# Paired row maxima in three PSUM banks: another grouping and order of the fills in causal attention heads

## The reference

```
score = einsum('bhqd,bhkd->bhqk', Q, K) / sqrt(8)
score = score - 1e10 * (1 - causal);  score = score - max(score, axis=-1)
weights = softmax(score);  attn = einsum('bhqk,bhkd->bhqd', weights, V)
```

## Time and profile before

| | |
|---|---|
| median of 3 runs | 1905.73 us (1902.89 to 1910.19) |
| profiled execution, its own time | 1905.62 us |
| its span, first to last instruction | 1903.8 us |
| mean granted clock of TensorE in it | 0.928 of full speed |
| the heads of layer 3 in the span | about 1403 to 1834 us |
| busy over the span | TensorE 87%, VectorE 75%, ScalarE 59% |

### The profile page before, as it was taken

One profiled execution on the slowest core, in us unless ns is written; L12 is line 12 of the kernel. 1 busy time (PEld: TensorE's weight loads), 2 busy tenths in 40 slices (PEclk: granted clock), 3 DMA queues, 4 the chain that ended last, 5 costly groups with the idle time before them and its releaser, 6 DMA issues. The chain is left out here.

```text
span 1903.8 us, 29255 instructions
## 1 busy us (share of the span) xinstructions
PE 1647.4 (87%) x10137; PEld 663.2 (35%) x10137; DVE 1428.8 (75%) x2698; ACT 1114.0 (59%) x2266; POOL 311.3 (16%) x462
## 2 busy tenths in 40 slices
PE   2899999999999995889997797893559998999987
PEld 1412222222222222434444544782322222323256
DVE  5689999999999944665555507656768999999825
ACT  3168888888888883332222244452206777777754
POOL 0101200000000100000000345543011222111123
PEclk8879999999999997899997899997658999999999
DMA  4101211121110012023223269951421111111132
GB/s 124 48 20 49 78 59 48 47 75 61 51 47 29 24 35 63 21 68 109 94 89 145 70 201 325 305 180 38 178 72 44 47 47 44 44 49 51 37 83 72
DMA packets 77378, 155.66 MB, mean 82 GB/s; under 512 B 17572, under 2 KB 34852, under 8 KB 73536
## 3 DMA queue, kind: packets, MB, share of 16 engines
q1 hardware_dynamic: 62630, 123.96, 20.1%
q0 software_dynamic: 14384, 29.29, 5.1%
q10 hardware_dynamic: 218, 0.55, 0.1%
HBM read 103.41 MB, written 48.89 MB: 80 GB/s over the span
## 5 line engine op out<-in xcount | busy, mean ns | idle before, releaser
L859 ACT ACTIVATE heads_probs<-heads_pS 128x512 f32<-128x512 f32 (+3 forms) x1664 | 819.8, 578 | 182.3 <-PE heads_pS L771 96.2
L883 DVE TENSOR_REDUCE heads_run_max<-heads_pM 128x1 f32<-128x1024 f32 x512 | 601.3, 1219 | 26.5 <-PE heads_pM L746 18.1
L790 PE MATMUL heads_pO<-heads_probs,heads_vh 128*32 128x512 f32 (+2 forms) x3328 | 445.9, 583 | 0.7 <-ACT heads_probs L859 0.7
L746 PE MATMUL heads_pM<-heads_ks,heads_qs 56*128 56x512 bf16 (+3 forms) x1040 | 319.5, 380 | 20.1 <-DVE heads_run_max L894 9.4
L771 PE MATMUL heads_pS<-heads_qs,heads_ks 59*128 59x512 bf16 (+3 forms) x1040 | 306.1, 368 | 2.4 <-DMA heads_qs<-heads_max_rows 1.6
L894 DVE TENSOR_REDUCE heads_run_max<-heads_pM 128x1 f32<-128x512 f32 x384 | 246.6, 684 | 16.5 <-PE heads_pM L746 14.2
L746 PE MATMUL heads_pM<-heads_k_first,heads_q_first 56*128 56x512 bf16 x624 | 193.2, 384 | 30.1 <-DVE heads_run_max L923 15.8
L771 PE MATMUL heads_pS<-heads_q_first,heads_k_first 59*128 59x512 bf16 x624 | 188.8, 377 | 4.6 <-ACT heads_probs L859 4.6
L771 PEld LDWEIGHTS heads_pS<-heads_qs,heads_ks 59*128 59x128 bf16 x1040 | 81.8, 93 | 266.9 <-ACT heads_probs L859 232.7
L891 DVE CUSTOM_DVE_ANT_0 heads_masked_out<-heads_pM,heads_mask_end 128x128 bf16<-128x128 f32 (+3 forms) x256 | 121.2, 486 | 13.1 <-PE heads_pM L746 8.2
L1410 ACT ACTIVATE top_act_gate<-top_pG 128x512 f32<-128x512 f32 x68 | 40.6, 597 | 137.2 <-PE top_pU L1366 137.2
(11 more groups left out here) (385 smaller groups left out, 2105.0 us busy)
## 6 DMA issues: line engine op xcount, KB each, us to landing
top_weights<-k_comb_dram SPq DMA_DIRECT2D x128, 128.0 KB, 3.0
second_w<-in_L_W_dram SPq DMA_DIRECT2D x12, 1024.0 KB, 11.7
k_hid_slots_dram<-k_zeros SPq DMA_DIRECT2D x8, 1152.0 KB, 4.4
k_h_slots_dram<-second_work SPq DMA_DIRECT2D x48, 192.0 KB, 2.9
second_work<-k_hid_slots_dram SPq DMA_DIRECT2D x48, 192.0 KB
heads_qs<-k_parts_dram SPq DMA_DIRECT2D x40, 192.0 KB
heads_ks<-k_parts_dram SPq DMA_DIRECT2D x80, 96.0 KB
k_parts_dram<-proj_part SPq DMA_DIRECT2D x12, 512.0 KB, 4.4
```

The source lines that it names most:

```text
L746: mm = pe.matmul(pM[:, bank_of(c, j, k), 0:w], qs[c % ROUND][rows, i * P:(i + 1) * P], ks[c % ROUND][rows, b * BLK:b * BLK + w], start=Tru ...
L790: mm = pe.matmul(pO[k * 32:k * 32 + VW, o:BLK], vh[c][:, t, at:at + VW], probs[u % 2][:, k * BLK + o:(k + 1) * BLK], start=first_chunk[u] ...
L859: act.activation(probs[u % 2][:, k * BLK + c0 - b * BLK:(k + 1) * BLK], pS[:, slot, 0:c1 - c0], ACT.Exp)\
L883: dve.reduce_max(run_max[:, i, blocks[0][0] // 2:blocks[0][0] // 2 + 1], both.rearrange("p k c -> p (k c)"), AX.X).then_inc(taken, 2)
```

## The change

Among the causal runs, two whole blocks of a query tile become one run: TensorE fills two neighbouring banks, and one `reduce_max` of VectorE reads 1024 columns. A third whole block stays a run of its own, and the masked block too. That gives 32 runs of 40 blocks: rows 0 to 3 masked; rows 4 to 7 single, masked; rows 8 to 11 pair, masked; rows 12 to 15 pair, single, masked. The last four rows are put in another order, written s for the single run, m for the masked one: pair 12, s12, pair 13, m12, pair 14, s13, pair 15, m13, s14, m14, s15, m15. `BLOCKS` is rounded up to a multiple of `FILLED` (40 to 42), so that a block has the same bank in every head, and the last take of a head adds the two missing counts. A pair always lies in banks 0 and 1. `LEAD` follows from the number of runs: 2 + 32 * 2 // 5 = 14. `upto`, by which the runs are spread over the units, becomes 0, 4, 7, 10, 13, 17, 20, 23, 26, 29, 32 (before 0, 5, 9, 13, 17, 21, 25, 29, 32, 37, 40).

```diff
--- before.py
+++ after.py
@@ -516,12 +516,20 @@
+    rows = []
     for i in range(NT):
         hi = (i + 1) * P if causal else T
         blocks = [(b, min(BLK, hi - b * BLK)) for b in range(NB) if b * BLK < hi]
-        each = 1 if causal else 2
-        for k in range(0, len(blocks), each):
-            runs.append((i, blocks[k:k + each], causal and k + each >= len(blocks)))
+        whole = blocks[:-1] if causal else blocks
+        rows.append([(i, whole[k:k + 2], False) for k in range(0, len(whole), 2)])
+        if causal:
+            rows[-1].append((i, blocks[-1:], True))
+    if causal:
+        singles = [run for row in rows[-TPB:] for run in row[1:]]
+        runs = [run for row in rows[:-TPB] for run in row]
+        runs += [run for n, row in enumerate(rows[-TPB:]) for run in (row[0], singles[n])] + singles[TPB:]
+    else:
+        runs = [run for row in rows for run in row]
     return units, runs
@@ -542,7 +550,7 @@
-    BLOCKS = before[-1]
+    BLOCKS = -(-before[-1] // FILLED) * FILLED
@@ -736,6 +744,7 @@
+                assert len(blocks) == 1 or bank_of(c, j, 0) + 1 < FILLED
@@ -878,10 +887,11 @@
                 dve.wait_ge(filled, n + 1)
                 at = [(BLOCKS * c + before[j] + k) % FILLED for k in range(len(blocks))]
-                if not causal:
+                last = BLOCKS - before[ITEMS] if j == ITEMS - 1 else 0
+                if len(blocks) == 2:
                     both = pM[:, at[0]:at[0] + 2, :]
                     dve.reduce_max(run_max[:, i, blocks[0][0] // 2:blocks[0][0] // 2 + 1], both.rearrange("p k c -> p (k c)"),
-                                   AX.X).then_inc(taken, 2)
+                                   AX.X).then_inc(taken, 2 + last)
@@ -889,9 +899,9 @@
-                                                     LOWEST, ALU.add, ALU.max, run_max[:, i, b:b + 1]).then_inc(taken, 1)
+                                                     LOWEST, ALU.add, ALU.max, run_max[:, i, b:b + 1]).then_inc(taken, 1 + last)
                             continue
-                        dve.reduce_max(run_max[:, i, b:b + 1], pM[:, bank, 0:w], AX.X).then_inc(taken, 1)
+                        dve.reduce_max(run_max[:, i, b:b + 1], pM[:, bank, 0:w], AX.X).then_inc(taken, 1 + last)
```

## The result

The changed kernel takes 1957.93 us (median of 4, 1956.61 to 1963.14), the kernel before in the same runs 1904.85 us. The ratio is 1.0287, 95% interval 1.0272 to 1.0301: slower by 2.9%. The forecast was 1954.6, 1920 to 1978.

A forecast was written before the change was run, and what follows sets the result against it. The causal heads were taken as bound by a loop of waits between TensorE and VectorE. Fifteen intervals of +2.97 us (44.6) and +4.3 for head 0 gave +48.9 on 1905.73: 1954.6 us, range 1920 to 1978.

The forecast's parts named there:

- The main term, the waits: Causal heads: a pair's two banks stay held until its maximum is over, 1.98 us from pair to pair.
- The list of stalls: VectorE's seven gaps between pairs, 0.23 to 0.62 us, and 0.28 behind the last pair: 3.09 us per head.
- the walk: One causal head followed through both engines' queues with the trace's times: 27.9 us per head, +2.97.
- the old waits: VectorE's standing time in a causal head of the kernel before: 2.19 us of 24.93.
- VectorE's saving: Eight pairs per causal head, 1.14 us each instead of 1.20 for two singles: 0.48 us saved per head.
- The boundary: A head's first three fills wait for the last head's last block; covered by 1.13 us, uncovered under 0.6 per head.
- the row 9: Work of 1.54 us that the shorter lead moves from before head 0's negation into the steady part.
- Head 0: Its maxima at clock 0.50: pair to pair 2.41 us, stalls 6.3, +4.3 us after the saving and shorter lead.
- The sum: Layer 3's causal heads: 15 intervals of +2.97 us, 44.6, and +4.3 before them, together +48.9 us.
- (a): Rival: TensorE's order hides most new waits in the causal heads; 25.0 to 25.9 us per head, 1916 us; chance 0.11.
- (b): Rival: TensorE refills bank 2 under each pair, so it ends faster, 1875 us; chance 0.06.
- (c): Rival: TensorE's clock falls as it stands inside units; 1986 us, or 2048 if all at half clock; chance 0.07.

The follow-up runs named there:

- e3: The changed kernel with pairs only in rows 12 to 15 and single blocks in rows 8 to 11 (36 runs): 1933.80 us, ratio 1.0141.
- e4: The changed kernel, pairs still filled as one run but taken by two maxima of 512 columns that each give their bank back: 1958.13 us, ratio 1.0276.
- e6: Pairs with four banks for the maxima and three for the ring, two pairs in a row, against the kernel before: 1924.05 us, ratio 1.0092.
- e1: The kernel before with only BLOCKS rounded from 40 to 42, single blocks, old order: 1909.02 us, ratio 1.0019.
- e2: The changed kernel with each pair split into two single-block runs, keeping its order and rounding (40 runs): 1917.02 us, ratio 1.0062.
- e8: The changed kernel with runs spread over the units, and the lead reckoned, by VectorE's time instead of by count: 1950.58 us, ratio 1.0232.
- e5: The kernel before, single blocks, with four banks for the maxima and three for the ring of scores: 1907.25 us, ratio 1.0008.
- e12: e11 with the runs spread over the units by VectorE's time: 1967.11 us on another chip, ratio 1.0057 to the kernel before.
- e11: Four banks, ring of three, eight pairs, each followed by two small runs, against the kernel before: 1972.24 us on another chip, ratio 1.0076.

## Why the prediction was right

**The main term, the waits.** The cycle from pair to pair was put at 1.98 us; it is 1.99. The stalls were to be 0.50, 0.36 and 0.23 behind masked blocks of 256, 384 and 512 columns; start to start they are 0.51 (1557.69 + 0.34 to 1558.54), 0.37 and 0.24. (The brackets show 0.08 less, since the instruction before is still ending.) Behind a masked block of 128 columns I had 0.62 and the two such gaps have 0.83 (1555.50 + 0.22 to 1556.55) and 0.82: there the fill came out of the queue, behind sums, later than the release. The list of stalls lacked that; the walk had it (pair 9 at 6.62, measured 6.64). Nothing merged with the old waits: VectorE stands 28.01 - 22.26 = 5.75 us of a steady head, and 3.09 and 2.19 make 5.28. e3 shows that the loss grows with the pairs, e4 that it is the joint fill and not the wide read, e6 that with a fourth bank about half of the pairs' cost is gone.

**The walk.** From the start of unit 8's sums (1549.91) the sums of units 0, 1, 4, 5, 6 and 7 were forecast at 4.93, 8.62, 18.63, 20.91, 23.6 and 26.0; measured 4.92, 8.61, 18.60, 20.87, 23.78 and 26.08. The next unit 8 was forecast at 27.9 and came at 28.01; the 0.1 it is short by comes in between units 5 and 6 (2.91 for 2.69), at the boundary of the heads. The mean over fourteen intervals is 28.26, because some heads are longer, as before (25.10 against the 24.93 that the walk was set against): the difference, 3.16, is 0.19 above the 2.97.

**VectorE's saving.** It is there and small: from a pair to what follows it is 1.14 us (1556.55 to 1557.69), and 1.21 in e4 with two maxima (1531.91 to 1533.12). e4 is as slow as the changed kernel, so this saving went into waiting. The larger figures, 0.15 per pair by durations and 1.0 us per head by cycles, are not borne out.

**The boundary.** I called it covered. By e1 it costs 0.26 us per head, 3.6 us: VectorE is covered, TensorE's queue isn't. The walk contained the wait for the last block, so the sum had it; the text that set it to nothing was wrong.

**The order.** I gave it no price of its own; with single blocks it costs about 8 us (e2 less e1). In the changed kernel it is inside the walk, which was made with that order. Lead and spread had no price either, beyond the row 9 that the lead moves; by e8 others are worth 7 to 10 us.

**Head 0.** Forecast +5.8 before the shorter lead, measured +6.6; the cycle at clock 0.50 was put at 2.41, and the starts at 1409.92 and 1412.34 are 2.42 apart. The difference is mostly the wait of 0.59 in front of the first pair, at 1407.50, which I left out. The row given for the clock, 1431 to 1435, lies behind head 0's negation (1424.6); 1408 to 1412 of the kernel after shows 0.50 inside head 0's maxima.

**The sum.** +48.9 forecast; the profiles give +51.0, the medians +53.1. By intervals: fourteen of 2.97 make 41.6 and were 44.3; the first, 2.97 less the 1.54 of the shorter lead, 1.4 and was 2.5; head 0's maxima 5.8 and were 6.6. Each term is short by a little, none by its kind.

**The rivals.** (a), merged waits, would have been a head under 25.9; the steady heads are 28.0. (b) needed a cycle near 1.5, against 1.99. (c) fell: the clock was 1.00 through the steady heads, with TensorE standing 1.1 us and more in fills. The Trainium skill's account of a clock that swings when PSUM banks are cycled (TensorE: Matmul & The Clock Gate, on psum-queue depth-cycling) isn't borne out by this stage.

**What stays open.** With four banks pairs still cost: 17 us in e6 over e5, some 9 in e12 over e5 by the ratios. The traces place it in VectorE's waits of 0.5 to 1.35 us for single fills; the two largest that were followed, 1.09 in e6 and 1.35 in e11, are fills placed behind a unit's sums, and e12, spread by time, has 1.35 again. No run took such a wait away alone, so which of the two (coarse release, or the place of the fills among the sums) makes it is not settled.

## What to carry to other kernels

When a producer and a consumer share a few buffers, count how many runs of the largest size fit. Two of three banks in one run leave no room for a second such run, and the cycle becomes the read until its release (1.28 us) plus the fill until the next read starts (0.71), 1.99 us here with 1.14 us of work in it. Where two such runs fit, as in e6, two reads followed each other without a wait (2.35 us for both). Before joining two reads to save a fixed cost, measure that cost start to start, not by durations (0.06 us against 0.15 here), and walk one period through both in-order queues with the release and ready times of the trace; that walk gave the steady head of this kernel to 0.1 us. A wait that the consumer does not notice can still cost: e1's, at the head of TensorE's queue, cost 3.6 us.

## What was not expected of the hardware

TensorE's granted clock stayed at 1.00 in 1550 to 1600 us with 39.32 of 50 us busy and fills that waited 0.86 to 1.18 us at four places of a head. It had stayed at 0.50 through head 0's fills, and here 0.94 as a mean of 1448 to 1452 us is the first window of 4 us above that, though the stage's first sums ran at 1439.75.
